# A delta-rule front in another order: small beta products, root and reciprocal for the norms, queries scaled on POOL, triangular blocks inverted by columns

## The chip, the core and the metric

The kernel runs on one core of one Trainium2 chip, in one launch. The metric is the device time of the whole program in microseconds, the median of several runs. The five engines run their own instruction lists and meet only in semaphores: PE (TensorE, matrix products), DVE (VectorE), ACT (ScalarE), POOL (GpSimd) and SP (SyncE, which here only starts transfers).

## The reference, cut to what matters

The program computes two transformer layers; four blocks follow each other, each added to x. Only the first part of the first block is touched: layer norm, projections, and the preparation of a delta-rule scan over 512 tokens of 8 batches with 4 heads of 32.

```
x = x + _L0_attn_ref(_layernorm(x), Wq, Wk, Wv, Wbeta, Wo, g_norm)
...
q = _l2norm(split(x @ Wq, Dk))          # t / norm(t) per token and head
k = _l2norm(split(x @ Wk, Dk))
v = split(x @ Wv, Dv)
beta = sigmoid(x @ Wbeta).transpose(0, 2, 1)
o = _delta_rule(q, k, v, beta)
# step:  pred = k_t S;  err = (v_t - pred) * b_t;  S = S + k_t err;  o_t = q_t S
```

The kernel does the scan in chunks of 32 tokens. Within a chunk the errors solve a triangular system with the matrix I + tril(beta k k^T, -1), so for each chunk, head and batch it needs the products k k^T and q k^T ("grams") and the inverses of the two 16 x 16 diagonal blocks of that matrix.

## The kernel before, in words

`delta_front` is the first phase of the program, followed by `delta_solve` (the rest of the triangular solve, which begins when every engine has left the front) and `delta_scan`. All instructions stand in the order of the code, per engine; there is no scheduler. B = 8 batches of 512 tokens, 16 chunks of 32 tokens, 4 heads.

The layout is partitions = 4 heads x 32. A batch goes through these steps:

- ACT `centre` (L358): four activations normalise x into `xn`; PE `transpose` (L420): four transpositions into a bank of PSUM; ACT `transposed` (L365): one copy to `xnT`.
- PE `project` (L431): products 128 x 512 for q, k, beta and v, in that order. For beta the four columns of the weight are repeated 32 times (`w_rep`, L319), so that its result lies as those of q, k and v do.
- DVE `to_tokens` (L257, L261, L263): transpositions in 32 x 32 blocks of q, k (`raw`), beta and v.
- ACT `tokens`: squares (L372), and the exponential for the sigmoid (L374). DVE `sum_squares` (L270) adds the squares of each token; POOL (L213) raises the sums to the power -1/2 (`inv_norm`).
- DVE `normalise` one batch later: k and q times `inv_norm` (L285, L286), transposed back (L288, L291) into `kqT`. DVE `sigmoid`: add one, reciprocal.
- PE `grams`, two batches later (L440): 64 products of 32 x 32 with 32 x 64 into one bank pair of PSUM (`gram_ps`), which ACT `grams` empties (L382) three batches later; PE's next grams wait for that (`gram_sb`).
- POOL `mask_keys` (L198) masks q k^T; POOL `mask_beta` (L204) lays beta into a lower triangle; DVE `mask` (L298) multiplies it with k k^T; ACT `cross` (L390) copies the off-diagonal quarter.
- SP stores the masked blocks to DRAM in eight transfers a batch (L148) and loads them back with one block a partition (L153).

Then DVE `invert` inverts the blocks of batches 0 to 3 and those of 4 to 7 (half 0, half 1), row after row: a product of row i with the finished inverse (L306) and a sum along it (L308), with i from 1 to 15. The masks of batches 6 and 7 stand between the rows of half 0. The inverses go to DRAM and back (L163, L465).

What sets the order: an engine's instructions run in the order written; `wait_ge` holds an engine at an instruction and all behind it. In iteration i of the batch loop ACT does grams(i-3), tokens(i), cross(i-3), centre(i+2), transposed(i+1); PE does project(i), transpose(i+1), grams(i-2); POOL mask_keys(i-3), the power for batch i, mask_beta(i-2); DVE to_tokens(i), sum_squares(i), normalise(i-1), sigmoid(i), mask(i-3).

Of the kernel before, what the change touches and what calls it, by code (L numbers as in the profile page):

```python
# [12 lines left out]
P = 128  # L13
# [85 lines left out]
def delta_front(nc, g, ins, scratch):  # L99
# [5 lines left out]
    with ExitStack() as ctx:  # L105
# [5 lines left out]
        w, w_beta, w_rep = sb("w_a", [P, 3, D]), sb("w_beta", [P, HA]), sb("w_rep", [P, HA, DA])  # L111
# [4 lines left out]
        norm2, inv_norm = sb("norm2", [P, 2, 2, CH]), sb("inv_norm", [P, 2, 2, CH])  # L116
        beta_rows, beta_mask = sb("beta_rows", [P, CH, DA]), sb("beta_mask", [P, CH, DA])
# [4 lines left out]
        own, w_loaded, w_ready, built, zeroed = sem("own"), sem("w_a_loaded"), sem("w_ready"), sem("built"), sem("zeroed")  # L122
# [5 lines left out]
        raw_ready, squared, norm2_ready, inv_norm_ready = made("raw_ready", 2), made("squared", 2), made("norm2_ready"), made("inv_norm_ready")  # L128
        v_ready, beta_raw, beta_exp, beta_ready = made("v_ready"), made("beta_raw"), made("beta_exp"), made("beta_ready")
        mask_ready, normed, kqT_ready = made("mask_ready"), made("normed", 2), made("kqT_ready")  # L130
# [39 lines left out]
        def _(pool):  # L170
# [28 lines left out]

            def mask_beta(b):  # L200
# [5 lines left out]
            for i in range(B + 3):  # L206
                if i >= 3:
                    mask_keys(i - 3)
                if i < B:
                    pool.wait_ge(norm2_ready.sem, norm2_ready.made(i, 0))  # L210
                    if i >= 2:
                        pool.wait_ge(normed.sem, normed.made(i - 2, 1))
# [9 lines left out]
        def _(dve):  # L222
# [28 lines left out]
            def to_tokens(b):  # L251
# [7 lines left out]
                if b >= 1:  # L259
                    dve.wait_ge(beta_exp.sem, beta_exp.made(b - 1, 0))  # L260
                dve.transpose(beta_rows[:, :, :], by_chunk(beta_bank)).then_inc(beta_raw.sem, 1)  # L261
                dve.wait_ge(proj_ps.sem, proj_ps.made(b, 3))
                dve.transpose(g.rhs[:, b, :, 0:DA], by_chunk(v_bank)).then_inc(v_ready.sem, 1)  # L263

            def sum_squares(b):
                for s in range(2):
                    dve.wait_ge(squared.sem, squared.made(b, s))
                    if b >= 2 and s == 0:
                        dve.wait_ge(inv_norm_ready.sem, inv_norm_ready.made(b - 2, 0))
# [11 lines left out]

            def normalise(b):
                k, q = g.rhs[:, b, :, DA:2 * DA], raw[:, b % 2, 0, :, :]
                dve.wait_ge(inv_norm_ready.sem, inv_norm_ready.made(b, 0))
                dve.tensor_tensor(k, raw[:, b % 2, 1, :, :], bc(inv_norm[:, b % 2, 1, :], DA), ALU.mult).then_inc(normed.sem, 1)  # L285
                dve.tensor_tensor(q, q, bc(inv_norm[:, b % 2, 0, :], DA), ALU.mult).then_inc(normed.sem, 1)  # L286
                dve.wait_ge(normed.sem, normed.made(b, 0))
                did(dve.transpose(g.kqT[:, b, :, 0, :], k))  # L288
                dve.wait_ge(normed.sem, normed.made(b, 1))
# [10 lines left out]
            def invert(half, rows):  # L300
                batches = slice(half * B // 2, (half + 1) * B // 2)
                for i in rows:
                    if i == 1:
# [5 lines left out]
                    if i == LB - 1:  # L309
                        row.then_inc(inv_ready[half], 1)  # L310
# [2315 lines left out]
```

## Time and profile before

| what | us |
|---|---|
| median of three runs (2010.74 to 2014.05) | 2012.79 |
| the profiled execution, its own time | 2014.68 |
| its span, first to last instruction | 2013.0 |
| of that, until DVE has done the last inversion step | 124.04 |
| the same, until the first inversion step | 88.32 |

The profile is one execution of its own. Its time stands 1.89 us above the median, so what is worked out from its rows is added to 2014.68 and the 1.89 taken off again. Mean granted TensorE clock: 0.927 of full speed. The page's slices are 50 us wide and show the front as the first two and a half of 40; the table of stretches and the timeline tell more.

### The profile page before, as it was taken

How to read it: one execution, taken by the hardware profiler on the slowest of the kernel's cores; microseconds unless marked ns; L12 is line 12 of the kernel's file. 1: busy time of each engine (PE TensorE's matmuls, PEld its weight loads, DVE VectorE, ACT ScalarE, POOL GpSimd, SP SyncE). 2: the span in 40 equal slices, each digit the busy share in tenths (PEclk: the TensorE clock that was granted, in tenths of full speed). 3: DMA queues.
4: the chain of work that ended last, by engine and by line, in shares of the span. 5: the costliest groups of instructions: out<-in, count | busy, mean ns of one | idle time of the engine just before them, and what ended most of it. 6: DMA issues, size and time to landing. Idle time of an engine off the chain costs nothing. (4 is left out here: it accounts for less than half of the span.)

```text
span 2013.0 us, 48064 instructions
## 1 busy us (share of the span) xinstructions
PE 1752.2 (87%) x18438; PEld 760.4 (38%) x18438; DVE 1587.1 (79%) x2988; ACT 1286.2 (64%) x2656; POOL 1104.3 (55%) x712
## 2 busy tenths in 40 slices
PE   6537857999999955977999999999999999999997
PEld 3337832233333344653442333333333333333334
DVE  7843577999999575437779898999989899998963
ACT  4403243888888710216884777777787877787785
POOL 8713541000000055331135888989888998989895
PEclk9769977899999956988997999999999999999998
DMA  1230045111111061117994232332323223232311
GB/s 48 36 51 3 1 145 190 46 49 39 48 42 46 13 200 51 50 54 265 374 405 128 65 86 74 76 82 68 86 65 85 73 78 82 68 86 65 85 29 42
DMA packets 194487, 180.14 MB, mean 89 GB/s; under 512 B 58740, under 2 KB 155124, under 8 KB 194052
## 3 DMA queue, kind: packets, MB, share of 16 engines
q1 hardware_dynamic: 185860, 170.01, 29.0%
q0 software_dynamic: 2944, 7.10, 1.1%
q8 instruction: 102, 1.67, 0.4%
q10 hardware_dynamic: 5504, 0.73, 0.2%
q14 instruction: 77, 0.63, 0.1%
HBM read 101.16 MB, written 75.26 MB: 88 GB/s over the span
## 5 line engine op out<-in xcount | busy, mean ns | idle before, releaser
L975 DVE TENSOR_REDUCE maxima_l<-max_l 128x1 f32<-128x512 f32 x1024 | 644.5, 692 | 81.2 <-PE max_l L1077 81.2
L1037 ACT ACTIVATE probs_l<-exp_l 128x512 f32<-128x512 f32 x1024 | 575.3, 595 | 204.7 <-PE exp_l L1088 195.3
L951 POOL TENSOR_TENSOR part_sums_l<-probs_l 128x1024 f32<-128x1024 f32 x256 | 605.2, 2364 | 117.1 <-ACT probs_l L1037 106.8
L1077 PE MATMUL max_l<-k_stack_l,q_stack_l 96*128 96x512 f16 x1024 | 399.5, 391 | 4.0 <-DVE pv_bank_l L967 3.3
L1088 PE MATMUL exp_l<-q_stack_l,k_stack_l 100*128 100x512 f16 x1024 | 390.3, 382 | 5.3 <-ACT probs_l L1037 2.9
L1279 DVE TENSOR_REDUCE maxima_l<-max_l 128x1 f32<-128x512 f32 x512 | 317.1, 683 | 16.6 <-PE max_l L1365 16.5
L1316 ACT ACTIVATE probs_l<-exp_l 128x512 f32<-128x512 f32 x512 | 279.2, 600 | 58.3 <-PE exp_l L1378 54.6
L1122 PE MATMUL pv_bank_l<-probs_l,v_ring_l 128*32 128x512 f32 x2048 | 273.8, 606 | 14.9 <-ACT probs_l L1037 14.9
L1077 PEld LDWEIGHTS max_l<-k_stack_l,q_stack_l 96*128 96x128 f16 x1024 | 100.1, 98 | 328.3 <-DVE maxima_l L975 272.7
L1793 POOL IOTA rows_e<- 128x32 int32 x1 | 0.2, 183 | 384.6 <-POOLq L26 384.6
L957 POOL TENSOR_TENSOR part_sums_l<-part_sums_l 128x512 f32<-128x512 f32 x128 | 162.9, 1273 | 10.0
L982 DVE TENSOR_REDUCE key_sums_l<-part_sums_l 128x512 f32<-128x1024 f32 x128 | 158.6, 1239 | 9.3 <-POOL part_sums_l L951 9.3
L1365 PE MATMUL max_l<-k_stack_l,q_stack_l 48*128 48x512 f16 x512 | 140.9, 409 | 19.7 <-DVE pv_bank_l L1268 8.9
L1088 PEld LDWEIGHTS exp_l<-q_stack_l,k_stack_l 100*128 100x128 f16 x1024 | 99.1, 97 | 155.5 <-ACT probs_l L1037 124.8
L1421 PE MATMUL pv_bank_l<-probs_l,v_ring_l 128*9 128x256 f32 x2048 | 146.7, 383 | 2.6 <-ACT pv_l L1323 2.0
L1378 PE MATMUL exp_l<-q_stack_l,k_stack_l 50*128 50x512 f16 x512 | 119.9, 388 | 0.7 <-ACT probs_l L1316 0.5
L1107 PEld LDWEIGHTS y_bank_l<-w_out,oT_l 128*128 128x128 f32 x512 | 96.9, 191 | 41.7 <-issue 4.6
L2003 ACT ACTIVATE midT_e<-midT_ps_e 128x512 f32<-128x512 f32 x40 | 23.9, 597 | 125.6 <-PE midT_ps_e L2070 125.6
L1107 PE MATMUL y_bank_l<-w_out,oT_l 128*128 128x128 f32 x512 | 98.7, 274 | 0.5 <-DVE oT_l L987 0.5
L2256 DVE SCALAR_TENSOR_TENSOR parts_g<-ring_ps_g,parts_g 128x512 f16<-128x512 f32 x128 | 81.4, 687 | 22.1 <-ACT parts_g L2294 22.1
L1365 PEld LDWEIGHTS max_l<-k_stack_l,q_stack_l 48*128 48x128 f16 x512 | 36.6, 93 | 148.1 <-DVE maxima_l L1279 86.0
L2335 PE MATMUL ring_ps_g<-xnT_g,w_qkv 128*128 128x512 f16 x384 | 87.3, 383 | 4.3 <-DVE parts_g L2256 2.9
(294 smaller groups left out, 2435.4 us busy)
## 6 DMA issues: line engine op xcount, KB each, us to landing
scratch_qk_l<-parts_g SPq DMA_DIRECT2D x128, 256.0 KB, 9.1
q_stack_l<-scratch_qk_l SPq DMA_DIRECT2D x192, 128.0 KB
k_stack_l<-scratch_qk_l SPq DMA_DIRECT2D x192, 128.0 KB
scratch_v_l<-v_g SPq DMA_DIRECT2D x16, 1024.0 KB
v_ring_l<-scratch_v_l SPq DMA_DIRECT2D x64, 256.0 KB, 3.3
scratch_stack_l<-parts_c SPq DMA_DIRECT2D x16, 384.0 KB, 3.6
q_stack_l<-scratch_stack_l SPq DMA_DIRECT2D x64, 96.0 KB, 2.2
k_stack_l<-scratch_stack_l SPq DMA_DIRECT2D x64, 96.0 KB, 2.3
```

Of the source, the lines that this page charges most:

```text
L951: pool.tensor_tensor(part_sums[:, i, h, :, :], probs[:, i, h, 0:2, :], probs[:, i, h, 2:4, :], ALU.add).then_inc(pair_sum.sem, 1)
L957: pool.tensor_tensor(both[:, 0, :], both[:, 0, :], both[:, 1, :], ALU.add).then_inc(key_sum.sem, 1)
L975: dve.reduce_max(maxima[:, s % 2, at % NT, at // NT:at // NT + 1], max_bank(n, at)[:, :], AX).then_inc(max_taken.sem, 1)
L982: dve.tensor_reduce(key_sums[:, HALVES_ADD_AT.index(at), :], both.rearrange("p a t -> p t a"), AX, ALU.add).then_inc(key_sum2.sem, 1)
L1037: act.activation(probs[:, i, at // NT, at % NT, :], exp_ps[at % 2][:, :], ACT.Exp, scale=a.scale).then_inc(prob_tile.sem, 1)
L1077: pe.matmul(max_bank(n, at)[:, :], qs[0:SHIFT_ROW, s % RING, h, k * P:(k + 1) * P], ks[0:SHIFT_ROW, s % RING, h, :], start=True, stop=True ...
L1088: pe.matmul(exp_ps[at % 2][:, :], ks[0:SHIFT_ROW + HG, slot, h, k * P:(k + 1) * P], qs[0:SHIFT_ROW + HG, slot, h, :], start=True, stop=Tru ...
L1107: ins = pe.matmul(y_bank[:, j * D:(j + 1) * D], oT[:, s % 2, j * P:(j + 1) * P], w_out[:, group, :], start=(group == 0 and j == 0), stop=( ...
L1122: ins = pe.matmul(pv_bank[hh * HEAD_ROWS:hh * HEAD_ROWS + W, :], vs[:, slot, j, hh, :], probs[:, i, hh, j, :], start=(j == 0), stop=(j == ...
L1279: dve.reduce_max(maxima[:, s % 2, half, k, hh:hh + 1], max_ps[bank(n, at)][:, :], AX).then_inc(max_taken.sem, 1)
L1316: act.activation(probs[:, i, HALVES * hh + half, k, :], exp_ps[bank(m, at)][:, :], ACT.Exp, scale=a.scale).then_inc(prob_tile.sem, 1)
L1365: pe.matmul(max_ps[bank(n, at)][:, :], qs[rows, s % RING, hh, k * P:(k + 1) * P], ks[rows, s % RING, hh, :], start=True, stop=True).then_i ...
```

## The change

Six things change, all in `delta_front`:

- beta: instead of one product with repeated weights, 64 products a batch (16 chunks x 4 heads) with 32 stationary columns of `xnT` and one column of the weight, so that beta comes out of PE with tokens in partitions; ACT takes its exponential from PSUM. DVE's transposition of beta and the repeated weights go. PE does q, k, v, then beta.
- norms: ACT takes the root of the sums (`roots`), DVE the reciprocal (`invert_norms`), at the head of its next iteration; POOL's power goes.
- the product of the queries with the reciprocal norms moves from DVE to POOL (`scale_queries`), behind `mask_keys`.
- ACT's iteration begins with the copy of the next batch's x and ends with the gram copies and cross copies.
- the blocks are inverted by columns: when column j is final, its outer product with the column of the matrix is taken off all later columns.
- the masks of batches 6 and 7 stand behind 5 and 8 columns of half 0.

The core of the diff:

```diff
@@ POOL
+            def scale_queries(b):
+                q = raw[:, b % 2, 0, :, :]
+                pool.wait_ge(inv_norm_ready.sem, inv_norm_ready.made(b, 0))
+                pool.tensor_tensor(q, q, bc(inv_norm[:, b % 2, 0, :], DA), ALU.mult).then_inc(q_normed.sem, 1)
...
             for i in range(B + 3):
                 if i >= 3:
                     mask_keys(i - 3)
-                if i < B:
-                    pool.wait_ge(norm2_ready.sem, norm2_ready.made(i, 0))
...
-                    pool.tensor_tensor(inv_norm[:, i % 2, :, :], norm2[:, i % 2, :, :],
-                                       g.minus_half[:, 0:2 * CH].rearrange("p (s c) -> p s c", s=2), ALU.pow).then_inc(inv_norm_ready.sem, 1)
+                if 1 <= i < B + 1:
+                    scale_queries(i - 1)
@@ DVE
-                dve.transpose(beta_rows[:, :, :], by_chunk(beta_bank)).then_inc(beta_raw.sem, 1)
-                dve.wait_ge(proj_ps.sem, proj_ps.made(b, 3))
                 dve.transpose(g.rhs[:, b, :, 0:DA], by_chunk(v_bank)).then_inc(v_ready.sem, 1)
...
+            def invert_norms(b):
+                dve.wait_ge(norm_ready.sem, norm_ready.made(b, 0))
+                dve.reciprocal(inv_norm[:, b % 2, :, :], norm[:, b % 2, :, :]).then_inc(inv_norm_ready.sem, 1)
...
-                dve.tensor_tensor(q, q, bc(inv_norm[:, b % 2, 0, :], DA), ALU.mult).then_inc(normed.sem, 1)
...
+                dve.wait_ge(q_normed.sem, q_normed.made(b, 0))
                 settle()
                 dve.transpose(g.kqT[:, b, :, 1, :], q).then_inc(kqT_ready.sem, 1)
...
-                    for_j = a_blocks[:, batches, i, 0:i].unsqueeze(2).broadcast_to([P, B // 2, i, i])
-                    did(dve.tensor_tensor(terms[:, :, 0:i, 0:i], for_j, inv[:, batches, 0:i, 0:i], ALU.mult))
+                    wide, low = j + 1, LB - 1 - j
+                    a_column = a_blocks[:, batches, wide:LB, j].unsqueeze(2).broadcast_to([P, B // 2, wide, low])
+                    row = bc(inv[:, batches, 0:wide, j], low)
+                    did(dve.tensor_tensor(terms[:, :, 0:wide, wide:LB], row, a_column, ALU.mult))
                     settle()
-                    row = dve.tensor_reduce(inv[:, batches, 0:i, i], terms[:, :, 0:i, 0:i], AX, ALU.add, negate=True)
+                    below = inv[:, batches, 0:wide, wide:LB]
+                    rest = dve.tensor_tensor(below, below, terms[:, :, 0:wide, wide:LB], ALU.subtract)
...
             for i in range(B + 1):
+                if i >= 1:
+                    invert_norms(i - 1)
                 if i < B:
                     to_tokens(i)
@@ ACT
+                act.wait_ge(proj_ps.sem, proj_ps.made(b, 3))
+                act.activation(g.beta[:, b, :], beta_bank[:, 0:CH], ACT.Exp, scale=-1.0).then_inc(beta_exp.sem, 1)
+
+            def roots(b):
+                act.wait_ge(norm2_ready.sem, norm2_ready.made(b, 0))
...
+                act.activation(norm[:, b % 2, :, :], norm2[:, b % 2, :, :], ACT.Sqrt).then_inc(norm_ready.sem, 1)
...
             for i in range(B + 3):
+                if i + 1 < B:
+                    transposed(i + 1)
+                if i < B:
+                    tokens(i)
+                if i + 2 < B:
+                    centre(i + 2)
+                if i < B:
+                    roots(i)
                 if i >= 3:
                     grams(i - 3)
-                if i < B:
-                    tokens(i)
...
                 if i >= 3:
                     cross(i - 3)
-                if i + 2 < B:
-                    centre(i + 2)
-                if i + 1 < B:
-                    transposed(i + 1)
@@ PE
+                for c in range(CH):
+                    for h in range(HA):
+                        last = pe.matmul(beta_bank[h * DA:(h + 1) * DA, c:c + 1], xnT[:, b % 2, c * DA:(c + 1) * DA], w_beta[:, h:h + 1],
+                                         start=True, stop=True)
+                last.then_inc(proj_ps.sem, 1)
```

How the order changes is seen best in the two engines' lists. On ACT, one iteration of the batch loop (batch 4: its squares and its exponential), before, from the gram copies of batch 1 to the copy of x of batch 5:

```order
L382 COPY gram<-gram_ps_a 128x512 x2
L372 ACTIVATE squares<-raw 128x512 x2
L374 ACTIVATE beta_d<-beta_rows 128x16
L390 COPY cross_d<-gram 16x16x16 x4
L358 ACTIVATE xn_a<-x_res,shift_a,rstd_a 128x128 x4
L365 COPY xnT_a<-xT_ps_a 128x512
```

and the same iteration after the change, with L381 the root and the lines 8 higher or so:

```order
L366 COPY xnT_a<-xT_ps_a 128x512
L373 ACTIVATE squares<-raw 128x512 x2
L375 ACT_TABLE_LOAD
L375 ACTIVATE beta_d<-beta_ps_a 128x16
L359 ACTIVATE xn_a<-x_res,shift_a,rstd_a 128x128 x4
L381 ACT_TABLE_LOAD
L381 ACTIVATE norm<-norm 128x32
L389 COPY gram<-gram_ps_a 128x512 x2
L397 COPY cross_d<-gram 16x16x16 x4
```

The copy of x moved from the end of the iteration to its head, the gram copies from its head to behind the root, and two loads of an activation table came in. On PE, the same batch before, from its q product to the grams of two batches earlier:

```order
L431 MATMUL q_ps_a<-xnT_a,w_a 128x512
L431 MATMUL k_ps_a<-xnT_a,w_a 128x512
L431 MATMUL beta_ps_a<-xnT_a,w_rep 128x512
L431 MATMUL v_ps_a<-xnT_a,w_a 128x512
L420 MATMUL xT_ps_a<-ident,xn_a 128x128 x4
L440 MATMUL gram_ps_a<-kqT_d 32x64 x64
```

and after the change:

```order
L437 MATMUL q_ps_a<-xnT_a,w_a 128x512
L437 MATMUL k_ps_a<-xnT_a,w_a 128x512
L440 MATMUL v_ps_a<-xnT_a,w_a 128x512
L445 MATMUL beta_ps_a<-w_beta,xnT_a 32x1 x64
L429 MATMUL xT_ps_a<-ident,xn_a 128x128 x4
L456 MATMUL gram_ps_a<-kqT_d 32x64 x64
```

v and beta changed places, and beta is 64 small products; the transpositions of the next x and the grams keep theirs behind all products of the batch.

## Rows read from the trace of the kernel before

**Rows 1.** Stretches: bounds and length in us, engines' busy us (instructions), granted clock, DMA.

```profile
33.74:88.32 54.58, 36.75 (x842) 23.24 (x846) 47.36 (x77) 31.61 (x73) 51.47 (x19) 0.85 0.18 24
88.32:124.04 35.72, 3.20 (x120) 2.96 (x112) 33.66 (x63) 2.68 (x6) 4.71 (x4) 0.50 0.37 56
```

**Rows 2.** Groups by line, front: busy us, mean ns of one, idle before.

```profile
L213 POOL TENSOR_TENSOR inv_norm<-norm,minus_half 128x32 f32<-128x32 f32 x8 | 46.0, 5744 | 1.6 <-DVE norm L270 1.6
L198 POOL TENSOR_TENSOR qk_d<-gram,upper 128x512 f32<-128x512 f32 x8 | 11.6, 1448 | 0.0
L204 POOL TENSOR_TENSOR beta_mask<-lower,beta_d 128x512 f32<-128x512 f32 x8 | 8.3, 1043 | 5.6 <-DVE a_mat L298 5.6
L257 DVE STREAM_TRANSPOSE raw<-q_ps_a 128x512 f32<-128x512 f32 x8 | 5.6, 694 | 0.9 <-PE q_ps_a L431 0.9
```

**Rows 3.** Timeline, 26 to 60 us: start us, duration us, instruction [idle before].

```profile
26.93 1.12 PE L431 MATMUL q_ps_a<-xnT_a,w_a 128*128 128x512 f32 x2 [1.78 <-ACT xnT_a L365]
...
41.41 0.56 ACT L365 COPY xnT_a<-xT_ps_a 128x512 f32<-128x512 f32 x1
41.88 1.06 ACT L382 COPY gram<-gram_ps_a 128x512 f32<-128x512 f32 x2
42.03 1.12 PE L431 MATMUL q_ps_a<-xnT_a,w_a 128*128 128x512 f32 x2 [2.23 <-ACT xnT_a L365]
...
44.71 1.02 PE L431 MATMUL v_ps_a<-xnT_a,w_a 128*128 128x512 f32 x2
...
45.57 0.60 PE L420 MATMUL xT_ps_a<-ident,xn_a 128*128 128x128 f32 x4
...
47.62 1.17 ACT L372 ACTIVATE squares<-raw 128x512 f32<-128x512 f32 x2 [4.68 <-DVE raw L257]
...
48.76 0.23 ACT L374 ACTIVATE beta_d<-beta_rows 128x16 f32<-128x16 f32 x1
48.89 1.63 ACT L390 COPY cross_d<-gram 16x256 f32<-16x256 f32 x4
...
50.55 1.65 ACT L358 ACTIVATE xn_a<-x_res,shift_a,rstd_a 128x128 f32<-128x128 f32 x4
...
52.71 2.08 PE L431 MATMUL q_ps_a<-xnT_a,w_a 128*128 128x512 f32 x2 [4.63 <-ACT xnT_a L365]
...
58.00 1.25 PE L431 MATMUL v_ps_a<-xnT_a,w_a 128*128 128x512 f32 x2
```

**Rows 4.** Timeline, PE: grams at either clock, and the solve's first products.

```profile
67.02 1.99 PE L440 MATMUL gram_ps_a<-kqT_d 32*32 32x64 f32 x128
...
80.03 3.63 PE L440 MATMUL gram_ps_a<-kqT_d 32*32 32x64 f32 x128 [5.38 <-DVE kqT_d L291]
...
128.01 6.54 PE L501 MATMUL y_ps_s<-rhs_s,weighted 32*32 32x64 f32 x256 [36.50 <-POOL weighted L531]
```

**Rows 5.** Timeline, PE and its weight loads (PEld): small products elsewhere.

```profile
215.51 0.74 PE L612 MATMUL pred_ps_r<-state,kqT_stage 32*32 32x32 f32 x64
216.10 0.74 PE L612 MATMUL o_ps_r<-state,kqT_stage 32*32 32x32 f32 x64
...
1301.91 0.16 PEld L1122 LDWEIGHTS pv_bank_l<-probs_l,v_ring_l 128*32 128x32 f32 x8 [0.24 <-issue]
```

**Rows 6.** Timeline, ACT: table loads in the scan and in the next block.

```profile
197.54 0.37 ACT L745 COPY o_r<-o_ps_r 128x256 f32<-128x256 f32 x1
197.92 1.28 ACT L735 ACT_TABLE_LOAD   x1
...
345.28 1.28 ACT L1316 ACT_TABLE_LOAD   x1
```

**Rows 7.** Timeline, DVE: the smallest and largest inversion product, half 1.

```profile
107.96 0.17 DVE L306 TENSOR_TENSOR terms<-a_blocks,inv_blocks 128x4 f32<-128x4 f32 x1
...
121.78 1.10 DVE L306 TENSOR_TENSOR terms<-a_blocks,inv_blocks 128x900 f32<-128x900 f32 x1
```

**Rows 8.** Timeline, SP's queue: issue of the last block loads.

```profile
103.55 1.66 SPq L153 DMA_DIRECT2D a_blocks<-scratch_blocks  x2
```

More of the change, by code:

```diff
@@ L298, in mask, with invert @@
                 dve.tensor_tensor(a_mat[:, b % 2, :, :], gram[:, b % 2, :, 0, :], beta_mask[:, :, :], ALU.mult).then_inc(a_ready.sem, 1)
-            def invert(half, rows):
+            def invert(half, columns):
                 batches = slice(half * B // 2, (half + 1) * B // 2)
-                for i in rows:
-                    if i == 1:
+                for j in columns:
+                    if j == 0:
                         dve.wait_ge(a_loaded[half], 16 * (B // 2))
-                    for_j = a_blocks[:, batches, i, 0:i].unsqueeze(2).broadcast_to([P, B // 2, i, i])
-                    did(dve.tensor_tensor(terms[:, :, 0:i, 0:i], for_j, inv[:, batches, 0:i, 0:i], ALU.mult))
+                    wide, low = j + 1, LB - 1 - j
+                    a_column = a_blocks[:, batches, wide:LB, j].unsqueeze(2).broadcast_to([P, B // 2, wide, low])
+                    row = bc(inv[:, batches, 0:wide, j], low)
+                    did(dve.tensor_tensor(terms[:, :, 0:wide, wide:LB], row, a_column, ALU.mult))
                     settle()
-                    row = dve.tensor_reduce(inv[:, batches, 0:i, i], terms[:, :, 0:i, 0:i], AX, ALU.add, negate=True)
-                    if i == LB - 1:
-                        row.then_inc(inv_ready[half], 1)
+                    below = inv[:, batches, 0:wide, wide:LB]
+                    rest = dve.tensor_tensor(below, below, terms[:, :, 0:wide, wide:LB], ALU.subtract)
+                    if j == LB - 2:
+                        rest.then_inc(inv_ready[half], 1)
                     else:
-                        did(row)
+                        did(rest)
                         settle()
@@ L317, in _ @@
             centre(0)
-            dve.wait_ge(w_loaded, 64)
-            dve.tensor_copy(w_rep[:, :, :], bc(w_beta[:, :], DA)).then_inc(w_ready, 1)
             centre(1)
@@ L336, in _ @@
             settle()
-            invert(0, range(1, 7))
+            invert(0, range(0, 5))
             mask(B - 2)
-            invert(0, range(7, 9))
+            invert(0, range(5, 8))
             mask(B - 1)
-            invert(0, range(9, LB))
+            invert(0, range(8, LB - 1))
             dve.wait_ge(inv_ready[0], 1)
-            invert(1, range(1, LB))
+            invert(1, range(0, LB - 1))
             dve.wait_ge(inv_ready[1], 1)
@@ L424, in project @@
                 pe.wait_ge(xT_sb.sem, xT_sb.made(b, 0))
-                taken = (raw_ready.made(b - 1, 0), raw_ready.made(b - 1, 1), beta_raw.made(b - 1, 0), v_ready.made(b - 1, 0))
-                sems = (raw_ready.sem, raw_ready.sem, beta_raw.sem, v_ready.sem)
-                weights = (w[:, 0, :], w[:, 1, :], w_rep[:, :, :], w[:, 2, :])
-                for n, (bank, lhsT) in enumerate(zip((q_bank, k_bank, beta_bank, v_bank), weights)):
+                for n, bank in enumerate((q_bank, k_bank)):
                     if b >= 1:
-                        pe.wait_ge(sems[n], taken[n])
-                    pe.matmul(bank[:, :], lhsT, xnT[:, b % 2, :], start=True, stop=True).then_inc(proj_ps.sem, 1)
+                        pe.wait_ge(raw_ready.sem, raw_ready.made(b - 1, n))
+                    pe.matmul(bank[:, :], w[:, n, :], xnT[:, b % 2, :], start=True, stop=True).then_inc(proj_ps.sem, 1)
+                if b >= 1:
+                    pe.wait_ge(v_ready.sem, v_ready.made(b - 1, 0))
+                pe.matmul(v_bank[:, :], w[:, 2, :], xnT[:, b % 2, :], start=True, stop=True).then_inc(proj_ps.sem, 1)
+                if b >= 1:
+                    pe.wait_ge(beta_exp.sem, beta_exp.made(b - 1, 0))
+                for c in range(CH):
[3 more added lines that the diff above has]
+                last.then_inc(proj_ps.sem, 1)
             def grams(b):
```

30 lines of the change are left out of this document (11 added, 19 removed).

## The prediction

> **What bounds the kernel now.** The change touches only the first phase, the delta front, so I read the busy time by stage first. From the q product of batch 3 at 33.74 us to the first inversion instruction at 88.32 us the front works on batches 3 to 7; from there to 124.04 us DVE inverts the 16 x 16 blocks nearly alone, and the solve behind it starts when DVE is done [rows 1]. So a microsecond of the front is a microsecond of the program, and 54.58 + 35.72 us are at stake.
>
> In the first of these stretches POOL is busy 51.47 of 54.58 us [rows 1]. The groups by line say with what: eight powers of -1/2 at 5.74 us each, beside 1.45 and 1.04 us a batch for the two masks [rows 2]. A batch cannot take less than 8.2 us on POOL. The timeline of one batch shows that POOL is not alone: PE waits 4.63 us for ACT's copy of the next x before it makes q at 52.71, and ACT had waited 4.68 us for DVE's transposition of q [rows 3]. One batch here takes 52.71 - 42.03 = 10.7 us. The reader is to see that the order on ACT decides: the copy of gram for batch i-3 stands directly behind the copy of x, before the squares of batch i.
>
> **The change, part by part.**
>
> *The handover between PE and ACT.* On PE a batch is q, k, (beta, v), transpositions of the next x, grams of batch i-2, and these grams wait until ACT has emptied the one gram bank of batch i-3. Before, ACT empties it at the head of its iteration. After the change ACT's iteration i begins with the copy of x for batch i+1, which waits for PE's transpositions, which stand behind all products of batch i; then come squares, exponential, centring, root, and only then the copies of gram i-3. PE's grams i-2 wait for these, and the products of batch i+1 are queued behind the grams. From batch 3 on PE and ACT therefore work in turns, not side by side. A period is the sum of both:
> PE: grams 1.99 [rows 4]; three large products, 44.71 - 42.03 = 2.68; transpositions 0.60 [rows 3]; the beta products.
> ACT: copy 0.56, squares 1.17, exponential 0.23, centring 1.65, gram copies 1.06 [rows 3], the root at 0.30 (an estimate, a little over the exponential on half as many elements), and two table loads.
>
> *Table loads.* Square, copy and the centring run under either table: the scan copies and squares around its roots, and its one load stands between a copy and the root [rows 6]. The root needs a load of 1.28 us behind a front that used the exponential, and the later exponential needs one again [rows 6]. Every iteration now has both in turn, so 15 loads of 1.28 us are added and the scan's one goes. The load starts 0.01 us behind the copy's end (197.54 + 0.37 to 197.92), so I add nothing to 1.28. Where ACT waits anyway a load is hidden (the one at 345.28 runs ahead of its exponential), but from the x copy to the gram copies ACT never waits in the new order, so both count: 2.56 us a period. The Trainium skill, "ScalarE: Activation LUTs", Table sets: the hidden batching unit, asks to do all the exps together and then all the sqrts, which is what this change does not do. Its section What ACT_TABLE_LOAD costs adds a drain of about 1.38 us to each load; the row shows no such gap. By the page a period would be 2.8 us longer and the sum about 11 us higher; I go by the row.
>
> ACT's part is 0.56 + 1.17 + 1.28 + 0.23 + 1.65 + 1.28 + 0.30 + 1.06 = 7.5 us.
>
> *The beta products.* One 128 x 512 product of 0.86 us becomes 64 products with 32 stationary columns and one moving column, each in two passes: 128 instructions. No row has this shape. The nearest with fewer moving columns, 64 instructions of 32 x 32 in 216.10 - 215.51 = 0.59 us, makes 1.2 us; the grams, 128 instructions with 64 columns, make 1.99 [rows 4, 5]. Both use 32 rows in four row groups, while the new ones take all 128 rows. If no two of the four column groups overlapped, it would be four times the first, 4.8 us. I take 2.0. The Trainium skill, "TensorE: Matmul & The Clock Gate", The mechanism, says that a weight load overlaps running matmuls only when the row group differs, which would favour the upper end; the trace shows eight loads of 128 x 32 started within 0.16 us in front of their matmuls [rows 5], which speaks for the lower.
>
> *PE's clock.* PE now rests through ACT's 7.5 us in each period. After 5.38 us of rest the grams at 80.03 ran at half speed, 3.63 instead of 1.99 [rows 4], and after 4.63 us the q product took 2.08 instead of 1.12 [rows 3]. Full speed came back near 58.00, 5.3 us after that restart [rows 3]. Small products bring it back too: of the 256 at 128.01 all at half speed would take 2 x 3.63 = 7.26 us, all at full speed 3.98; they took 6.54, so the last fifth ran at full speed, after some 5.7 us [rows 4]. In the new loop the restart begins with grams (3.63) and q (half, +0.86): the rest is at full speed. That adds 1.64 + 0.86 = 2.5 us.
>
> Period: 1.99 + 2.68 + 2.0 + 0.60 + 7.5 + 2.5 = 17.3 us.
>
> *Where the loop starts and ends.* Batches 0 to 2 have no gram copies: an iteration of ACT is 7.5 - 1.06 = 6.5 us, against 33.74 - 26.93 = 6.8 between two q products now [rows 1, 3]. PE's beta products add 2.0 - 0.86 = 1.1 to each of the three batches, of which the shorter iterations and the power that goes give back most; I take 34.6 for q of batch 3, 0.9 later than now. Then: products, beta, transpositions 5.3, to 39.9; ACT 7.5, and 0.6 because the squares of batch 3 wait for DVE's reciprocal of the norms and the transposition of q, to 48.0; grams at half speed, q of batch 4 at 51.7; two periods, 86.3; one without centring (there is no batch 8), 15.6: q of batch 7 at 101.9.
> Behind it: q at half speed 1.9, k 0.9, DVE's transposition of k 0.7 [rows 2], square 0.6, load, exponential, load, root, gram copies (4.2): gram 4 ready at +8.5. Then POOL, whose list is gram mask, query scaling, beta mask, so that the scaling of batch 6 stands behind the mask of gram 4: 1.45 + 1.3 (scaling, not in the trace; between the 1.04 of the beta mask and the 1.45 of the gram mask [rows 2]), DVE transposition 0.7, sigmoid 0.4 (two small instructions, an estimate), mask 0.7 like the other passes over 512 elements: about +13. Then POOL beta mask 1.04, gram mask 1.45, scaling 1.3, and on DVE transposition and mask 1.4: +18.25. The first inversion is at 101.9 + 18.25 = 120.15 instead of 88.32: +31.8 us. DVE loses the beta transposition and the query product, about 1.4 us a batch, but it waits for ACT and POOL in this loop, so I count nothing.
>
> *Inversion by columns.* 30 instructions a half remain. Sums: rows of i x i, 4 x 1240 = 4960 elements twice; columns of (j+1)(15-j), 4 x 680 = 2720 elements twice. Per element: (1.10 - 0.17) / (900 - 4) = 1.04 ns [rows 7]. Saved: 2 x 2240 x 1.04 = 4.7 us a half. The new first operand has steps of 16 elements; no row shows that stride in this operation, so the bounds are no cost and a doubled product, 2.8 us; I take none, since the reduction already writes with that step and fits the same line. In the first half the saving runs into a wait: the second half needs the blocks of batch 7, and SP's last loads are issued until 103.55 + 1.66 = 105.2 [rows 8], while the second half starts at 107.96 [rows 7]. SP's eight stores a batch keep their pace, so at most 2.7 us can be had there, less the landing; I take 1.0. Together -5.7 (bounds -1.8 and -7.4).
>
> *At nothing:* w_rep's copy and its semaphore (the x moments cover it); the memsets; the scan's table load (0 to -1.3, ACT has slack there).
>
> Sum: 31.8 - 5.7 = +26. The profiled execution took 2014.68 us (span 2013.0), 1.9 over the median 2012.79: 2014.68 + 26 - 1.9 = 2039.
>
> **The rivals.**
> 1. *PE's clock stays full.* The period is 14.8; q of batch 7 at 34.6 + 5.3 + 8.1 + 2.0 + 29.6 + 13.1 = 92.7, first inversion 17.4 later: +21.8 - 5.7 = +16, 2029. With beta at 1.2 and the larger inversion gain it is 2021. Against it: both rests in rows 3 and 4 were shorter and ended at half speed.
> 2. *Half speed through the whole loop.* Products 1.75, beta 1.0, transpositions 0.3 more in three periods and some 2 in the tail: +12, 2051. For it: the grams at 80.03 and their successors stayed slow; against it the recovery in rows 3.
> 3. *Column groups do not overlap* (the skill's rule above): beta 4.8 us, 2.8 more in three early batches and four of the loop: +20, 2059.
> 4. *Faster.* POOL's power was the pace and goes; if ACT's gram copies did not stand in the way of PE (PE a bank ahead), ACT's own list would set the pace: 7.5 + 1.63 for the four cross copies = 9.2 us a batch [rows 3]. Then q of batch 7 is at 34.6 + 3 x 9.2 + 7.6 = 69.8, the inversion at 87.2, -1.1 - 5.7 = -7: 2006. It decides as soon as four periods stay under about 10.5 us. For it speaks POOL's 51.47 of 54.58 us; against it the single gram bank and the order on ACT and PE: the wait is in the code, whatever the durations.
>
> **How the numbers follow.** Forecast 0.50; full clock 0.17; half speed throughout 0.12; beta serial 0.11; faster 0.10, of which a third could end within 0.2% (4 us, what a measurement here can tell from no change). So faster 0.07, same 0.03, slower 0.90. The range runs from rival 1 with its better bounds, 2021, to rival 3, 2059; what it leaves out is the faster case and the combined worst.
>
> **What would show it.** Right: in the changed profile PE's grams wait for ACT's gram copies 7 us and more in four batches; ACT has sixteen table loads of 1.28 us in the front; q products stand 16 to 18 us apart from batch 4 on; granted clock of half in their first part; the second half of the inversion takes 11 to 12 us instead of 16.1; DVE waits for a block load between the halves. Wrong: if q products stand 9 to 11 us apart, ACT and PE overlap after all and the sign is in doubt; if the beta products take over 4 us, rival 3 holds; if the inversion saves nothing, the strided operand costs.

## The result and the profile after

The changed kernel took 2043.24 us, the median of four runs (2045.81, 2062.6, 2040.2, 2040.67), against 2013.33 for the kernel before on the same chip: a ratio of 1.0175, 95% interval [1.0131, 1.0218]. The profiled execution is the first of the four, with a span of 2044.1 us.

Where the time went is read at four marks that both traces have: the first inversion step on DVE, the solve's first copy on POOL, the first instruction of the scan, and the end.

| mark | before | after | difference |
|---|---|---|---|
| first inversion step | 88.32 | 119.61 | +31.3 |
| start of the solve (POOL's copy to rhs_s) | 125.57 | 152.91 | +27.3 |
| start of the scan (POOL's memset of eps_r) | 190.40 | 220.33 | +29.9 |
| end of the span | 2013.0 | 2044.1 | +31.1 |

So the front gives up 31 us before the inversion, the inversion by columns gives 4 back, and some 4 more are lost behind. The stretches of the changed kernel (columns as in [rows 1]) are batches 3 to 7, the inversion and the solve:

```profile
37.34:119.61 82.27, 46.54 (x1587) 34.77 (x1582) 37.51 (x69) 49.39 (x95) 21.50 (x19) 0.75 0.13 18
119.61:151.20 31.59, 0.00 (x0) 0.00 (x0) 27.04 (x62) 1.77 (x5) 2.62 (x2) 0.50 0.40 61
152.91:220.33 67.42, 51.67 (x3072) 49.45 (x3072) 16.26 (x40) 18.76 (x32) 21.38 (x25) 0.89 0.09 11
```

POOL, busy 51.47 of 54.58 us before [rows 1], has 21.50 of 82.27 now: the powers are gone. But now no engine is full in this stretch: PE is busy 46.54 us and ACT 49.39, and their sum, 95.9, is near the length. Two engines that are each busy for over half of a stretch and together for little more than all of it take turns. The timeline of PE and ACT over one period shows it:

```profile
49.28 3.64 PE L456 MATMUL gram_ps_a<-kqT_d 32*32 32x64 f32 x128 [7.35 <-ACT gram L389]
52.85 2.08 PE L437 MATMUL q_ps_a<-xnT_a,w_a 128*128 128x512 f32 x2
...
56.81 1.24 PE L445 MATMUL beta_ps_a<-w_beta,xnT_a 128*32 128x1 f32 x128
57.98 0.66 PE L429 MATMUL xT_ps_a<-ident,xn_a 128*128 128x128 f32 x4
58.67 0.59 ACT L366 COPY xnT_a<-xT_ps_a 128x512 f32<-128x512 f32 x1 [7.80 <-PE xT_ps_a L429]
59.28 1.15 ACT L373 ACTIVATE squares<-raw 128x512 f32<-128x512 f32 x2
60.45 1.28 ACT L375 ACT_TABLE_LOAD   x1
...
61.83 1.63 ACT L359 ACTIVATE xn_a<-x_res,shift_a,rstd_a 128x128 f32<-128x128 f32 x4
63.48 1.28 ACT L381 ACT_TABLE_LOAD   x1
64.77 0.23 ACT L381 ACTIVATE norm<-norm 128x32 f32<-128x32 f32 x1
64.91 1.05 ACT L389 COPY gram<-gram_ps_a 128x512 f32<-128x512 f32 x2
...
66.11 3.30 PE L456 MATMUL gram_ps_a<-kqT_d 32*32 32x64 f32 x128 [7.47 <-ACT gram L389]
69.34 1.13 PE L437 MATMUL q_ps_a<-xnT_a,w_a 128*128 128x512 f32 x2
```

From 58.67 to 65.96 ACT works through its list while PE stands. From 66.11 PE works, and ACT, once its cross copies are done, stands until PE's transpositions come; before the x copy of 58.67 it had stood 7.80 us. One period is 69.34 - 52.85 = 16.5 us, where the kernel before took 10.7 [rows 3]. The waits of 34 to 100 us give the same from both sides (total us, times, longest):

```profile
PE gram_ps_a L456 <- ACT gram L389: 28.2, 4, 7.5
ACT xnT_a L366 <- PE xT_ps_a L429: 24.0, 5, 7.8
```

The four long waits of PE in this window are 7.35, 7.47, 7.47 and 5.94 us.

### The profile page after: what moved, and what is told of

Read it like the earlier page. It is cut to its first block and busy times, and to the rows that moved or that the text cites. A ratio compares the mean times of both kernels' runs of the same rounds, so it can differ in the third digit from the quotient of the medians.

```text
span 2044.1 us, 50080 instructions
## 1 busy us (share of the span) xinstructions
PE 1767.7 (86%) x19446; PEld 773.4 (38%) x19446; DVE 1568.5 (77%) x2979; ACT 1306.5 (64%) x2678; POOL 1067.2 (52%) x712
```

## The experiments

Two questions: is it this taking of turns that costs 31 us, or the operations themselves (table loads, small products, clock)? And why do four runs of one kernel lie 22 us apart? Each ratio is to the kernel before, run beside it on the same chip.

| kernel | us, runs | ratio to before, 95% |
|---|---|---|
| e1 gram copies first | 2029.71 (2013.74 to 2035.42), 4 | 1.0087 [1.0055, 1.0120] |
| e2 no table loads | 2042.03 (2028.53 to 2055.96), 4 | 1.0162 [1.0120, 1.0204] |
| e3 inversion by columns alone | 2007.07 (2003.66 to 2009.49), 6 | 0.9986 [0.9973, 0.9999] |
| e5 = e1 + e2 | 2012.12 (2009.9 to 2028.45), 4 | 1.0030 [1.0000, 1.0060] |
| e6 small beta products alone | 2036.55 (2034.52 to 2044.11), 5 | 1.0123 [1.0104, 1.0143] |
| e7 = e1, one large beta product | 2007.99 (2003.04 to 2013.82), 12 | 0.9976 [0.9965, 0.9988] |
| e8 = e7, exponential on POOL | 2014.40 (2013.0 to 2021.39), 11 | 1.0014 [1.0002, 1.0026] |
| e9 before + 504 products | 2053.55 (2033.07 to 2063.17), 6 | 1.0207 [1.0186, 1.0228] |
| e10 = e6 + 32 products | 2012.35 (2008.37 to 2016.86), 12 | 1.0000 [0.9987, 1.0013] |
| e11 before + 252 products | 2011.19 (2007.13 to 2015.75), 12 | 0.9996 [0.9983, 1.0009] |
| e12 after + 32 products | 2038.88 (2032.47 to 2040.97), 5 | 1.0125 [1.0110, 1.0140] |
| e13 = e1 + 32 products | 2007.30 (2002.34 to 2011.24), 12 | 0.9974 [0.9963, 0.9985] |

### e1: the changed kernel with ACT's gram copies first

```diff
             for i in range(B + 3):
+                if i >= 3:
+                    grams(i - 3)
                 if i + 1 < B:
                     transposed(i + 1)
...
-                if i >= 3:
-                    grams(i - 3)
```

> The changed kernel with one edit: in ACT's iteration the gram copies of batch i-3 go first, ahead of the copy of x for batch i+1. Theory (PE and ACT take turns because PE's grams wait for gram copies that stand behind the root): PE no longer waits there, the q products of batches 4 to 7 stand 9 to 10.5 us apart instead of 15.6, the first inversion step falls from 119.6 to about 93 to 98 us, and the program takes about 2018 to 2023 instead of 2043. Rival (the table loads, or a PE that runs at half clock, make the period, whatever the order): the products stay 14 us and more apart and the time within 5 us of 2043.

The first inversion step is at 85.44 us, 34 earlier than in the changed kernel, by moving two copies, 1.05 us together, in each batch. Of these 34 us, 4.3 are a later start of the loop in the profiled execution of the changed kernel (q of batch 3 at 37.34 against 33.03); e12 and e13 below, which start alike, differ by 32.6. PE's waits for the gram copies fall to a third, and ACT is the full engine (waits, then stretch, of 33.03 to 85.44):

```profile
PE gram_ps_a L456 <- ACT gram L389: 10.1, 6, 3.4
```
```profile
33.03:85.44 52.41, 41.31 (x1494) 30.49 (x1493) 38.49 (x72) 49.15 (x95) 21.16 (x20) 0.83 0.20 27
```

49.15 of 52.41 us busy: now ACT's own list sets the pace. So the turns are what cost the 31 us of the front. Both expected figures were missed: the first inversion came earlier than 93 to 98 us, and the median, 2029.71, lies above 2018 to 2023, for it does not follow the front: the profiled run took 2013.74, the three others 2026 to 2036.

### e2 and e5: no table loads

Both leave the root out: a square of the same size stands in its place, so that one activation table serves throughout.

```diff
-                act.activation(norm[...], norm2[...], ACT.Sqrt)
+                act.activation(norm[...], norm2[...], ACT.Square)
```

> The changed kernel with the root replaced by a square (the norms come out wrong; same size, no second activation table), so that the 15 added table loads go. Theory (ACT and PE in turns, so each load on ACT between the copy of x and the gram copies counts in full): 2.56 us a batch from batch 3 on and part of that before, 13 to 18 us in all: about 2027. Rival (loads run while ACT waits for something else): 0 to 4 us, 2039 or more.

> Both edits of the two runs beside it: gram copies first, and a square for the root (the norms come out wrong). Theory: with the turns broken ACT's own list sets the pace; without 2.56 us of loads it is 6.7 us a batch, and DVE with about 7 us or POOL's handovers come next, so q products 7.5 to 9 us apart, first inversion step at 82 to 90, about 2005 to 2013, no slower than the kernel before. Rival (the half clock of PE rules): above 2020.

In e2 the first inversion step came at 108.64 us, 11.0 earlier than with the loads, somewhat less than the expected 13 to 18. In the serial loop the loads count nearly in full: from q of batch 3 to q of batch 7 it is 9.1 us shorter, where four periods of 2.56 us are 10.2 (q ran at half speed in three of e2's periods). In e5, behind e1's order, the first inversion came at 86.81, no earlier than e1's 85.44. Part of this is the start, q of batch 3 at 37.19 instead of 33.03; from there to the first inversion e5 took 49.6 us and e1 52.4, so that only 2.8 us remain of the loads. There ACT, relieved, waits 10.2 us for PE's transpositions, and PE is the later of the two. The total of e2 nevertheless did not fall. Its solve took 88.6 us instead of 65 to 67, with stalls of PE that its trace lays to "issue": PE waited for nothing that the profile shows. That was not in the prediction, and it set the second question.

### e3: the inversion by columns alone

```diff
-                    did(dve.tensor_tensor(terms[:, :, 0:i, 0:i], for_j, inv[:, batches, 0:i, 0:i], ALU.mult))
+                    did(dve.tensor_tensor(terms[:, :, 0:wide, wide:LB], row, a_column, ALU.mult))
```

> The kernel before with only the inversion by columns. Theory: the second half of the inversion takes 13.1 us as it does in the changed kernel, not 16.1, and the first half saves little because the second waits for the last block load (issued to 105.2 us): 3 to 4.5 us faster than before, about 2009. Rival (the waits for block loads take all of it): within 1.5 us of before.

The solve started at 122.35 us, 3.2 earlier than before, and the total is 2.6 us lower: this part of the change is worth what the trace of its stretch says, though by the interval only just beyond the noise. Of the two parts that were run alone (this one and the small products) it is the one that gains; the norms and the scaling on POOL were not run alone.

### e6, e7, e8: beta alone, the rest without it, and ACT's last loads

e6 is the kernel before with this in place of the large product (and the exponential read from PSUM); e7 is e1 with the large product back; e8 is e7 with the exponential of the sigmoid on POOL.

```diff
+                for c in range(CH):
+                    for h in range(HA):
+                        last = pe.matmul(beta_bank[h * DA:(h + 1) * DA, c:c + 1], xnT[...], w_beta[:, h:h + 1], ...)
```
```diff
+                pool.tensor_tensor(g.beta[:, b, :], inv_e[:, :], beta_rows[:, :, 0], ALU.pow)
```

> The kernel before with one part of the change alone: beta as 64 one-column products a batch, ordered q, k, v, beta, and its exponential read from PSUM; copies, orders of the engines and the column-free inversion stay as before. Theory (handover): in the changed kernel the front is long because ACT's gram copies come behind the x copy, the squares and the centring; the small products themselves cost PE 1.25 us a batch less one large product of 0.9 us and save DVE one transposition, so this kernel should have its first inversion at 86 to 90 us (before 88.3) and a median of 2008 to 2016, at the fast end within 3 us of before. Second theory (code): the 128 instructions that each batch adds to PE's stream lead PE, in some executions, to fetch the code of the solve again, as the solve of the kernel with Square for Sqrt showed (88.6 us in place of 65 to 67): then some of its runs lie 15 to 25 us above the others, while the kernel before, beside it, spreads by no more than 8. If it spreads like the kernel before, the spread has another source than the small products alone. Clock: if the one-column products bring the half clock, batches 1 and 2 show q at 1.5 us rather than 0.9.

> The kernel with ACT's gram copies first in each turn, but beta again as one large product with DVE's transposition of its 16 columns; all else of the change stays. Handover theory: the front is as in the gram-first kernel, q products 8 to 10 us apart, first inversion at 83 to 88, the solve's start at 116 to 121 (before 125.6), and the whole 2002 to 2010. Code theory adds: without the small products no run lies 15 us or more above the fastest, while the gram-first kernel had three of four there. If the spread stays, it belongs to something else that both share (the new order of ACT's stream, or the inversion by columns, which alone had no spread).

> The last kernel with the exponential of the sigmoid made on POOL as a power of 1/e (128x16, by the row of L191's power some 2.9 us), the sigmoid on DVE one batch later, so that ACT loads a table no more within a batch (two loads of 1.28 us fewer in each). Theory that ACT's own 8.9 us a batch sets the pace once the grams are copied first: ACT falls to about 6.1 us a batch, the q products come 7 to 8 us apart, bounded next by DVE, and the first inversion is at 75 to 82, the whole 1995 to 2005. Rival: the blocks' stores and loads on SP (some 5 us a batch, behind the grams) and POOL's queue (2.9 us more a batch, masks behind it) take the place, the first inversion stays at 84 to 88 and the whole within 3 us of the last kernel.

e6 lost 23 us, and not in the front: the first inversion is at 90.07 and the solve starts at 127.47, 1.9 later than before, but the scan starts at 215.04, 24.6 later. All five runs lie at 2034 or above, not only some of them, as the second theory had it; and the q products of batches 1 and 2 took 2.08 and 1.12 us, so its sign for the clock came in one of two. PE's list of the solve is a loop of four equal passes, each for a pair of batches. In the timeline of PE in e6 (start, length, what, idle before) each pass begins with a product from rhs_s:

```profile
129.92 3.63 PE L501 MATMUL y_ps_s<-rhs_s,weighted 32*32 32x64 f32 x126 [36.91 <-POOL weighted L531]
...
155.90 1.99 PE L501 MATMUL y_ps_s<-rhs_s,weighted 32*32 32x64 f32 x128 [0.82 <-DVE rhs_d L569]
...
175.23 3.39 PE L501 MATMUL y_ps_s<-rhs_s,weighted 32*32 32x64 f32 x126 [7.94 <-issue]
179.09 0.27 PE L501 MATMUL y_ps_s<-rhs_s,weighted 32*32 32x64 f32 x2 [0.47 <-issue]
...
183.69 0.30 PE L501 MATMUL y_ps_s<-rhs_s,weighted 32*32 32x64 f32 x5 [2.05 <-issue]
...
195.44 2.02 PE L501 MATMUL y_ps_s<-z_s,weighted 32*32 32x64 f32 x127 [1.87 <-issue]
199.48 0.41 PE L501 MATMUL y_ps_s<-z_s,weighted 32*32 32x64 f32 x10 [2.02 <-issue]
200.70 1.99 PE L501 MATMUL y_ps_s<-rhs_s,weighted 32*32 32x64 f32 x128 [0.81 <-DVE rhs_d L569]
```

The third pass stalls at nearly the same places as the first, most of them some 127 matmuls apart, and takes 33.4 us from the end of the second pass's products (167.29) to 200.70; the kernel before takes 12.6 (163.49 to 176.06). The queue that carries instructions says what it waits for, first in the solve of the kernel before, then of e6 (packets, MB):

```profile
q8 instruction: 6, 0.10, 0.6%
```
```profile
q8 instruction: 16, 0.26, 1.3%
```

One pass over the loop is six packets of 16 KB; ten more were fetched in e6, nine of them between 167.29 and 200.70. PE loaded the loop's code a second time; what the packets beyond six were is not shown. e7, without the small products, has no such run among twelve and is 0.24% under before. The products' own time is not the reason: the 128 small matmuls of a batch, with their weight loads, take 1.24 us.

e8 took two loads of 1.28 us out of each batch of ACT and came out slower than e7, its first inversion at 92.06 instead of 85.66. The timeline of POOL, and that of DVE under it, shows a new ring, 9.3 us long in four batches running:

```profile
74.64 1.04 POOL L215 TENSOR_TENSOR beta_mask<-lower,beta_d 128x512 f32<-128x512 f32 x1 [3.15 <-DVE a_mat L308]
75.64 2.91 POOL L209 TENSOR_TENSOR beta_d<-inv_e,beta_rows 128x16 f32<-128x16 f32 x1
78.52 1.25 POOL L200 TENSOR_TENSOR qk_d<-gram,upper 128x512 f32<-128x512 f32 x1
79.73 1.04 POOL L205 TENSOR_TENSOR raw<-raw,inv_norm 128x512 f32<-128x512 f32 x1
83.92 1.05 POOL L215 TENSOR_TENSOR beta_mask<-lower,beta_d 128x512 f32<-128x512 f32 x1 [3.15 <-DVE a_mat L308]
```
```profile
78.65 0.72 DVE L272 STREAM_TRANSPOSE beta_rows<-beta_ps_a 128x512 f32<-128x512 f32 x1 [2.14 <-POOL beta_d L209]
...
83.15 0.63 DVE L308 TENSOR_TENSOR a_mat<-gram,beta_mask 128x512 f32<-128x512 f32 x1
```

POOL's mask (74.64) stands in front of its power (75.64). DVE's transposition of beta into the one buffer `beta_rows` waits until the power has read it (78.65), the masking stands behind that transposition in DVE's list (83.15), and POOL's next mask waits for the masking (83.92). Mask and power make 3.9 us of the ring, DVE's list the rest. The rival stated for it held in kind, but the loss is larger than its 3 us (6.4, with the first inversion 6.4 later), and the ring runs over POOL and DVE, not over POOL's queue alone.

### e9, e10, e11: how much code, or where

```diff
+            for n in range(504):     # e10: 32, on top of e6; e11: 252
+                pe.matmul(beta_bank[0:DA, 0:1], xnT[:, 1, 0:DA], w_beta[:, 0:1], start=True, stop=True)
```

> The kernel before, beta as one large product, with 504 one-column products of PE added in one place behind the last grams, where PE does nothing until the solve (91.5 to 125 us in the trace of before): as many instructions ahead of the solve as the small beta products add. What they compute is read by nothing. Theory that the length of the code ahead of the solve's loop decides: the solve takes 85 to 90 us in place of 65 (its third pair loads the loop's code again: some 16 packets on PE's instruction queue in the solve rather than 6), and the whole is 2030 to 2045 in most runs, with the first inversion where it is in before. Rival, that the small products act by what they do in the batches (their clock, their PSUM bank, their place between v and the transpositions): the solve stays at 64 to 68 us and the whole at 2008 to 2017.

> The kernel with the small beta products alone (2036.55, solve 87.5 us in its profiled run), with 32 more one-column products behind the last grams, read by nothing: 128 instructions, or half of a 16 KB packet, so that the solve's loop lies half a packet later in the code. If the loop's place within a packet decides, the solve is back at 64 to 68 us and the whole at 2010 to 2020. If it is the amount of code that has gone before, or its timing, the solve stays at 85 to 90 us in most runs and the whole at 2030 to 2045.

> The kernel before with 252 such products behind the last grams, half as many as the small beta adds: the loop lies some 4 packets later rather than 8. If the effect needs the full length or one place in the code, this stays like before (solve 64 to 68, whole 2008 to 2017); if any code more brings it now and then, some of the runs lie 15 to 25 us above the others; if it grows with the length, the solve takes some 75.

e10 decides: 32 further products, which compute nothing that is read, take e6 from 2036.55 to 2012.35, and its twelve runs lie within 8.5 us. More code made it faster, so neither the amount nor what the small products do in the batches is the cause, but where the loop lies. The stalls of the first pass give the place, since they come once a packet, 127 matmuls apart: in e6 after 377, 504, 631 and 758 of the pass's 768, which puts a packet's start 381 - 377 = 4 matmuls before the loop; worked out in the same way it is 12 in e11, 20 in before and 67 in e10. The loop returned for its code only where it begins about 4 matmuls behind a packet's start: shown by the traces of e2 and e6, and supported by the times of the other kernels with that place (the changed kernel, e1, e5, e9), whose profiled runs did not do it. No other place than these four was tried.

e9 was partly spoilt: its products all write one column and took 53.92 us at half clock (granted 0.50 throughout), instead of the 9.8 us that 1.24 us for 128 would make, so the solve started 21 us late:

```profile
91.53 53.92 PE L457 MATMUL beta_ps_a<-w_beta,xnT_a 128*32 128x1 f32 x1008
```

Its profiled run (2033.07) is before plus these 21 us, with a solve of 67.4 us; the five others lie 18 to 30 us above it, which is the size of a second code load, but none of them has a trace. The place is that of e6, without its products in the batches. By the times of those five, what the place does holds here too; the expectation foresaw the second load, but from the length of the code, which e10 rules out.

### e12, e13: the place mended in the changed kernel and in e1

The edit is e10's 32 products, on the changed kernel (e12) and on e1 (e13).

> The changed kernel with 32 more one-column products, read by nothing, behind its last grams, where PE does nothing for over 30 us; they lay the solve's loop half a 16 KB packet later in PE's code. If the changed kernel's loss of 31 us is in the front (first inversion at 119.6 us rather than 88.3) and the code's place adds only now and then, the median falls little, to 2036 to 2042, the front stays (inversion 118 to 121) and no run lies at 2060. If the code's place were a main part of the median, it would come to 2015 to 2030.

> The changed kernel with ACT's gram copies first in each turn and with the same 32 products behind the last grams: both causes taken away, all else of the change kept. If the two are all there is, the median is 2004 to 2010 (without the 32 products 2029.71, of which one run was 2013.74), all runs within 10 us of each other, and the solve takes 64 to 68 us; 2 to 8 us under the kernel before. If a third cause is in the small products themselves, it stays over 2013.

e12 keeps the loss: first inversion at 116.81, a little under the expected 118 to 121, median 2038.88, no run over 2041. So 27 us of the changed kernel's loss remain whatever the code's place; the changed kernel's run at 2062.6 lies as far above its others as a second load costs, though that run has no trace. e12 and e13 differ only in the place of ACT's gram copies: 116.81 against 84.17 us at the first inversion, 2038.88 against 2007.30 in the whole. These 31.6 us are what the turns cost, and the rest of the change gives 4.6 back. e13 has both causes away and is 0.26% faster than before, with twelve runs within 9 us. Its stretches, batches 3 to 7 and the solve:

```profile
31.98:84.17 52.19, 40.41 (x1465) 29.47 (x1464) 39.00 (x73) 48.92 (x94) 20.87 (x20) 0.83 0.20 27
...
118.05:182.11 64.06, 50.33 (x3072) 48.40 (x3072) 16.38 (x40) 18.79 (x32) 21.36 (x24) 0.90 0.09 11
```

e7 and e13 cannot be told apart (intervals above): either beats both kernels, and the small products bring nothing.

## Why the prediction was right, point by point

- **The handover.** Right, and tested by e1. It said that PE's grams wait "7 us and more in four batches": they waited 7.35, 7.47, 7.47 and 5.94, the last without a centring, as its own sum had it. The q products of batches 3 to 7 stand 15.5, 16.5, 15.6 and 14.6 us apart, against 17.1, 17.3, 17.3 and 15.6, so its sign "16 to 18 us apart" held for one of the three periods from batch 4 on. The four periods were 5.1 us too large: 3.0 in the beta products, 0.6 in PE's other products, and 1.5 on ACT, whose list from the x copy to the end of the gram copies took 7.15, 7.29, 7.29 and 5.76 us; the wait of 0.6 us for DVE in the first period did not occur.
- **The beta products.** Mis-sized: 1.24 us a batch, beside the 2.0 taken and next to the lower bound of 1.2. In four periods this is 3.0 of the 5.1 us.
- **Table loads.** Right: 1.28 us, both in each period, and e2 gave 11.0 us back. They follow without a gap: the centring of 45.00 ends at 46.64, the load starts at 46.65.

```profile
45.00 1.64 ACT L359 ACTIVATE xn_a<-x_res,shift_a,rstd_a 128x128 f32<-128x128 f32 x4
46.65 1.28 ACT L381 ACT_TABLE_LOAD   x1
```

  The Trainium skill, "ScalarE: Activation LUTs", What ACT_TABLE_LOAD costs, adds a drain of about 1.38 us; no load in this front shows one.
- **PE's clock.** Right in kind: grams of 3.64 us after the rest (half speed, as in [rows 4]), and q at 2.08. The granted clock is 0.50 from 49.28 to 52.85. Later speed came back sooner: from 66.11 to 69.34 the granted clock is 0.56 and behind it 1.00, with grams of 3.30 us and q at 1.13, and q took 1.61 and 1.14 at 84.98 and 99.57. The prediction took q at half speed every time; this is the 0.6 us of the other products.
- **Where the loop starts.** q of batch 3 came at 37.34 instead of 34.6. The grams before it stood 1.41 us on "issue", which the prediction did not have, and batches 1 and 2 had slow q products (1.50 and 1.65 instead of 1.12). The stall is also in e12, which has the same front (1.19); the slow products are not (1.12 and 1.13, and q of batch 3 at 32.99), so they belong to the execution.
- **The tail of the front.** From q of batch 7 to the inversion 20.0 us instead of 18.25 (its terms up to gram 4 add up to 8.3, where it wrote 8.5). The chain that it added up was shorter than forecast, done on DVE at 116.17, 16.6 us behind q; the step that ends in "The first inversion is at" left out SP. The blocks of batch 3 are loaded behind the eight stores of batch 4, whose mask was only done at 110.97, so that DVE waits 3.45 us for them (before: none), and 2.34 us once more for batch 7 between the halves. SP's queue, then DVE:

```profile
111.00 4.74 SPq L148 DMA_DIRECT2D scratch_blocks<-a_mat  x8
115.78 0.45 SPq L153 DMA_DIRECT2D a_blocks<-scratch_blocks  x1
```
```profile
119.61 0.26 DVE L306 TENSOR_TENSOR terms<-inv_blocks,a_blocks 128x60 f32<-128x60 f32 x1 [3.45 <-DMA a_blocks<-scratch_blocks]
...
137.92 0.26 DVE L306 TENSOR_TENSOR terms<-inv_blocks,a_blocks 128x60 f32<-128x60 f32 x1 [2.34 <-DMA a_blocks<-scratch_blocks]
```

- **Inversion by columns.** Mis-sized: half 1 (batches 4 to 7) took 13.1 us (137.92 to 150.99) where 11.4 stood and 16.1 was before. The product's new operands, counted as nothing, are the cause. For the same 252 elements the product and the subtraction of the changed kernel differ (by form; mean ns last):

```profile
L306 DVE TENSOR_TENSOR terms<-inv_blocks,a_blocks 128x252 f32<-128x252 f32 x2 | 1.2, 586 | 0.1
...
L309 DVE TENSOR_TENSOR inv_blocks<-inv_blocks,terms 128x252 f32<-128x252 f32 x2 | 0.8, 422 | 0.1
```

  From 60 to 256 elements the product goes from 0.26 to 0.59 us, 1.68 ns an element, the subtraction from 0.22 to 0.42, 1.02 ns; 2720 elements at 0.66 ns more are 1.8 us, the whole difference, and inside the bound of 2.8 that was stated. Whether the step of 16 elements costs this is not shown: the product also spreads both operands over the block, where that of before spread one, and the two were not tried apart.
- **The sum.** The start of the loop (2.7 us late), the four periods (5.1 short) and the tail (1.8 long) nearly cancelled, so that the first inversion came at 119.61 where 120.15 was forecast. The turns are not luck, but that the figure came out so close is. The solve was forecast to start at 125.57 + 26.1 = 151.7 and started at 152.91. The profiled execution should have taken 2014.68 + 26 = 2040.7 us and took 2045.81: of these 5 us, 1.2 are there at the solve's start, 2.6 in the solve (67.4 us, in part at half speed in its first two passes) and 1.2 behind it, which the prediction left untouched. In e12, with the loop at another place in the code, the solve took 63.5.
- **The rivals.** The fourth put a kernel without the handover at "9.2 us a batch" and 2006 us; e13, in which it is gone, has ACT busy 48.92 of 52.19 us, its q products 8.1, 9.9, 9.3 and 7.3 us apart, and 2007.30. The third fell with the 1.24 us. The first two bounded the clock on both sides, and it lay between (the second's parts add up to 11, not 12). No rival and no term spoke of PE's code; in e6 this alone is 23 us.

## What to carry to other kernels

Before an engine's list is put in another order, ask of each single buffer who empties it and what now stands in front of that copy: two copies, a microsecond together, moved behind the squares, the two table loads and what lies between, made two engines take turns and cost 31 us. When an edit changes the number of an engine's instructions, look in the trace for "issue" waits and instruction packets in loops that it does not touch, and at the spread of several runs, and try a few idle instructions more before you judge the edit.

## What the runs showed of the hardware

- A loop of PE with a body of six 16 KB packets of code took 6 packets for its four passes in before, e10 and e13, but in e2 and e6 stalled for its code again in its third pass (16 packets in the solve), for 22 us. By their times, kernels with the loop about 4 matmuls behind a packet's start did so in some executions and not in others (e1 ran at 2013.74, with no such stall in its trace, and at 2035.42, without a trace); why the third pass, and why not always, stays open.
- 128 matmuls with 128 x 32 weights and one moving column take 1.24 us, 9.7 ns each with their weight loads, at full granted clock (1.00), when they go to 16 columns in each of four partition groups. The same shape with one weight block, always into one column, took 34 ns each at full clock (64 in 2.19 us in e10) and 53.5 at half clock (1008 in 53.92 us in e9, granted 0.50). Whether the column or the weights make the difference was not tried apart.
- A product on DVE of two operands spread over the block, one of them with a step of 16 elements, took 1.68 ns an element where a subtraction of the same size took 1.02, and a product with one spread operand in the kernel before 1.04 [rows 7].
